# Down and layer 2 on a transposed residual: a four-layer conditioned stack on one NeuronCore

## What is computed

```python
x = x + (einsum('bct,bcd->bdt', x, w0[a]) + bias[a][:, :, None])          # layer 0, 8 tables of 64x64
h = silu(x @ Wg + lora_g(x)) * (x @ Wu + lora_u(x))                       # layer 1, 512 -> 2048, rank 16, adapter a
x = x + (h @ Wd + lora_d(h))                                              #   "down", 2048 -> 512
x = x + (x @ W.T + scal[b] * (x @ A[b].T) @ Bm[b].T)                      # layer 2, 512 -> 512, rank 16, adapter b
x = x + einsum('bct,bcd->bdt', x, w3[c])                                  # layer 3, 200 tables of 64x64
```

## Time and profile before

| | us |
|---|---|
| median of three runs (765.55 to 767.71) | 766.35 |
| the profiled execution, as timed | 767.69 |
| its span, first to last instruction | 765.9 |

### The profile page before, as it was taken

How to read it: one execution, slowest core, us unless ns; L and a number is a source line. 1 busy time by engine, 2 the same in 40 slices (tenths; PEclk the granted TensorE clock), 3 DMA queues, 4 the chain that set the end, 5 groups by cost and what they waited for, 6 DMA issues and landing times.

```text
span 765.9 us, 10652 instructions
## 1 busy us (share of the span) xinstructions
PE 727.8 (95%) x3626; PEld 606.9 (79%) x3626; DVE 601.1 (78%) x1010; ACT 284.8 (37%) x508; POOL 255.3 (33%) x489
## 2 busy tenths in 40 slices
PE   6779889999999999989899999999999999899997
PEld 4547678888888888878778888888888888788886
DVE  7975768797878778799898979787888877766675
ACT  3445523333424333434353334242434333134232
POOL 4724231515223232350327162534425231241100
PEclk9979999999999999999999999999999999999999
DMA  7366520313212121203723232221212061212112
GB/s 209 87 81 194 164 80 29 104 37 108 83 56 83 55 84 56 83 27 111 248 59 109 71 103 73 70 86 58 89 55 85 28 192 32 79 29 70 42 55 83
DMA packets 65941, 66.02 MB, mean 86 GB/s; under 512 B 31712, under 2 KB 48096, under 8 KB 65888
## 3 DMA queue, kind: packets, MB, share of 16 engines
q1 hardware_dynamic: 57248, 45.92, 19.9%
q0 software_dynamic: 7296, 19.41, 8.7%
q10 hardware_dynamic: 1344, 0.02, 0.1%
HBM read 56.94 MB, written 8.39 MB: 85 GB/s over the span
## 4 chain that ended last, share of the span: by engine, by line
PE 84%; DVE 10%; issue 2%; ACT 2%; DMA 1%; POOLq 0%; POOL 0%; ACTq 0%; DVEq 0%
PE bank L1376 36%; PE bank L1474 22%; PE bank L1384 7%; PE bank L1633 6%; PE bank L1483 4%; PE bank L1622 2%; PE bank L1326 1%; PE bank L1599 1%; PE bank L1639 1%; DVE XC L882 1%; PE bank L1650 1%; PE bank L1611 1%; DVE hid L1001 1%; PE bank L1353 1%; DVE hs L1007 1%
## 5 line engine op out<-in xcount | busy, mean ns | idle before, releaser
L1376 PE MATMUL bank<-XC,WC 128*128 128x512 f32 x1344 | 332.9, 394 | 6.7 <-DVE tmp L975 2.2
L1376 PEld LDWEIGHTS bank<-XC,WC 128*128 128x128 f32 x1344 | 245.5, 190 | 54.8 <-issue 4.7
L1474 PE MATMUL bank<-wds,hs 128*128 128x512 f32 x768 | 187.6, 394 | 6.6 <-DVE X L1017 3.3
L1474 PEld LDWEIGHTS bank<-wds,hs 128*128 128x128 f32 x768 | 142.9, 190 | 35.8 <-DVE wds L960 3.8
L398 POOL DMA_INDIRECT BR<-in_L_cond_Bu_dram,boffs x64 | 71.9, 1124 | 265.7 <-DVE BL L954 251.1
L398 POOL DMA_INDIRECT BR<-in_L_cond_Bg_dram,boffs x64 | 76.1, 1189 | 95.2 <-DVE BL L954 80.2
L620 ACT ACTIVATE hs<-hid 128x512 fp32r<-128x512 f32 x64 | 40.3, 630 | 164.4 <-DVE hid L1001 111.4
L1017 DVE TENSOR_TENSOR X<-bank,X 128x512 f32<-128x512 f32 x128 | 86.5, 686 | 17.5 <-PE bank L1474 15.3
L614 ACT ACTIVATE hid<-hid 128x512 f32<-128x512 f32 x48 | 30.4, 633 | 148.4 <-DVE hid L984 75.9
L1384 PEld LDWEIGHTS bank<-UT,BL 128*128 128x128 f32 x512 | 76.4, 190 | 10.0 <-issue 2.1
L1384 PE MATMUL bank<-UT,BL 128*128 128x256 f32 x512 | 81.9, 283 | 1.3 <-ACT hid L611 1.3
(11 more groups left out here) (152 smaller groups left out, 827.9 us busy)
## 6 DMA issues: line engine op xcount, KB each, us to landing
RW<-in_L_cond_Wg_dram SPq DMA_DIRECT2D x16, 512.0 KB, 4.4
RW<-in_L_cond_Wu_dram SPq DMA_DIRECT2D x16, 512.0 KB, 5.1
RD<-in_L_cond_Wd_dram SPq DMA_DIRECT2D x16, 512.0 KB, 3.5
out_dram<-XR SPq DMA_DIRECT2D x16, 256.0 KB, 2.0
X<-in_x_dram SPq DMA_DIRECT2D x8, 256.0 KB, 6.2
udp<-in_x_dram SPq DMA_DIRECT2D x8, 256.0 KB, 4.5
x1park<-RD SPq DMA_DIRECT2D x8, 256.0 KB, 4.2
x2park<-X SPq DMA_DIRECT2D x8, 256.0 KB, 2.5
```

Of the source, the lines that this page charges most:

```text
L1376: last = nc.tensor.matmul(psum[:, :], WC[:, t, left, a, k, :], XC[:, right, b, k, :], start=(first and k == 0 and n == 0), stop=(k == 1 an ...
L1474: last = nc.tensor.matmul(psD[j % 2][:, :], hs[:, f, a, j * P:(j + 1) * P], wds[:, f, b, :], start=(f == 0 and n == 0), stop=(f == 1 and n ...
```

## The change

- The residual lies with features on partitions everywhere behind layer 0. `down` swaps its operands (Wd tile as weights, 512 tokens as moving operand), and `evict` adds into XA, which is the transposed x1 that the block products read anyway. `wd_high`, `wd_low`, the Bd splits and the W2, A2 transposes read their raw tile with a step of four floats (`by_feature`), since feature 4o+k sits in block k.
- Layer 2 takes x2 from there: `transposes2` is gone, `xt_high` and `xt_low` split 128x1024 from SBUF; `lora_down` has 12 matmuls of 256 columns in place of 6 of 512.
- Identity in the weights: `add_identity` now runs before any `place_w0`, so all pairs need only a bias (even pairs on ACT, odd ones on DVE); `w2_identity` (unit 15) and `w3_identity` (unit 14) on DVE. `x3_sum` and `y_sum` are gone; `x3_high` and `x3_low` read PSUM, which stays taken until both have read, and `y_out` on ACT copies layer 3's result out.
- `park_x1` stores the transposed tile in pieces of 512 bytes and waits for `xr_copy(p)` (`s_xr`), where it waited for the bias add. `load_d(0)` no longer waits for these stores. T blocks of the first half get their own place in XB. The warm-up is 12 matmuls of 128 columns, and SBUF names change (XR, X1 to XA, XB).

```diff
                 def park_x1(p):
-                    sp.wait_ge(s_x1b, p - HP + 1)
-                    sp.dma_start(x1park[p - HP, :, :], x1s[p % 2]).then_inc(s_x1st[p % 2], 16)
+                    sp.wait_ge(s_xr, p + 1)
+                    at = slice((p - HP) * P, (p - HP + 1) * P)
+                    sp.dma_start(x1park[:, :, at], XB[:, :, at]).then_inc(s_x1st, 16)
...
                         sp.wait_ge(s_tr, PAIRS)
-                        for s in range(2):
-                            sp.wait_ge(s_x1st[s], 16 * HP // 2)
...
                 def place_w0(p, cols):
                     if p == 0:
-                        pool.wait_ge(s_ident, 1)
-                        pool.wait_ge(s_w0, 32)
+                        pool.wait_ge(s_w0i, 1)
                         pool.wait_ge(s_zero, 1)
...
-                for g in range(2):
-                    cols += adapters(8 * g, 8)
-                    for p in range(4 * g, 4 * g + 4):
+                for n, count in ((0, 4), (4, 4), (8, 8)):
+                    cols += adapters(n, count)
+                    for p in range(n // 2, (n + count) // 2):
...
                 def x1_bias(p):
                     act.wait_ge(s_l0, p + 1)
-                    if p == HP:
-                        act.wait_ge(s_x1, HP)
-                    if p >= HP + 2:
+                    if p == 0:
+                        act.wait_ge(s_bias, 1)
+                    if p >= 2:
                         act.wait_ge(s_tr, p - 1)
-                        act.wait_ge(s_x1st[p % 2], 16 * ((p - HP) // 2))
-                    nc.scalar.activation(x1_of(p), psD[p % 2][:, :], ACT.Identity, bias=bias[:, p:p + 1]).then_inc(s_x1b, 1)
...
-                        nc.scalar.activation(wds[:, f, 0, :], RD[:, f, :], ACT.Copy).then_inc(s_wdh, 1)
+                        nc.scalar.activation(wds[:, f, 0, :].rearrange("p (k o) -> p k o", k=KT), by_feature(RD[:, f, :]),
+                                             ACT.Copy).then_inc(s_wdh, 1)
...
                 def xt_high(d):
-                    for q in range(2):
-                        act.wait_ge(c_tr, 2 * d + q + 1)
-                        if d >= 2 and q == 0:
-                            act.wait_ge(c_l2, 2 * d - 2)
-                        nc.scalar.activation(x2t[d % 2][:, 0, :, q * P:(q + 1) * P],
-                                             bank[q][:, :].rearrange("p (k t) -> p k t", k=KT), ACT.Copy).then_inc(c_xh, 1)
+                    act.wait_ge(s_x2, 2 * d + 2)
+                    if d >= 2:
+                        act.wait_ge(c_l2, 2 * d - 2)
+                    nc.scalar.activation(x2t[d % 2][:, 0, :, :], x2_of(d), ACT.Copy).then_inc(c_xh, 1)
...
+                def x3_high(d, q):
+                    act.wait_ge(c_l2, 2 * d + q + 1)
+                    if d >= 2:
+                        act.wait_ge(c_l3, 2 * (d - 2) + q + 1)
+                    nc.scalar.activation(x3s[d % 2][q][:, 0, :], psD[q][:, :], ACT.Copy).then_inc(c_x3h, 1)
...
+                def w3_high(d, q):
+                    if d == 0 and q == 0:
+                        act.wait_ge(s_w3i, 2)
+                    if d >= 1:
+                        act.wait_ge(c_l3, 2 * (d - 1) + q + 1)
+                    for half in range(2):
+                        rows = slice(half * POS, (half + 1) * POS)
+                        last = nc.scalar.activation(w3bd[q][rows, 0, rows], w3raw[rows, 2 * d + q, :], ACT.Copy)
+                    last.then_inc(c_w3h, 1)
...
+                def y_out(d, q):
+                    act.wait_ge(c_l3, 2 * d + q + 1)
+                    if d >= 2:
+                        act.wait_ge(c_out[d % 2][q], 16 * (d // 2))
+                    nc.scalar.activation(y[d % 2][q], psR[q][:, :], ACT.Copy).then_inc(c_y, 1)
...
+                    dve.wait_ge(s_w0, 32)
+                    tab0 = w0tab.rearrange("p c f -> p (c f)").rearrange("p (n d) -> p n d", d=POS)
+                    nc.vector.tensor_tensor(tab0, tab0, ident2[:, :].unsqueeze(1).to_broadcast([P, ADAPTERS, POS]),
+                                            ALU.add).then_inc(s_w0i, 1)
+                def w2_identity():
+                    dve.wait_ge(s_w2ld, 16)
+                    for k in range(KT):
+                        own_block = w2_raw[:, k, k * P:(k + 1) * P]
+                        last = nc.vector.tensor_tensor(own_block, own_block, ident[:, :], ALU.add)
...
+                    at = slice(half * HP, (half + 1) * HP)
+                    nc.vector.tensor_tensor(w3raw[:, at, :], w3raw[:, at, :],
+                                            ident2[:, :].unsqueeze(1).to_broadcast([P, HP, POS]), ALU.add).then_inc(s_w3i, 1)
...
-                def x1_sum(p):
+                def x1_bias(p):
                     dve.wait_ge(s_l0, p + 1)
-                    nc.vector.scalar_tensor_tensor(out=X1[:, p, :], in0=psD[p % 2][:, :], scalar=bias[:, p:p + 1],
-                                                   in1=X1[:, p, :], op0=ALU.add, op1=ALU.add).then_inc(s_x1, 1)
+                    if p >= 2:
+                        dve.wait_ge(s_tr, p - 1)
+                    nc.vector.tensor_scalar(x1s[p % 2], psD[p % 2][:, :], bias[:, p:p + 1], None, ALU.add).then_inc(s_x1[p % 2], 1)
...
+                    if unit == ALL - 2:
+                        w3_identity(0)
+                        w3_identity(1)
+                    if unit == ALL - 1:
+                        w2_identity()
...
                 for d in range(DUOS):
                     if d + 1 < DUOS:
+                        x2_sum(d + 1, 0)
+                        x2_sum(d + 1, 1)
                         xt_low(d + 1)
-                    x3_sum(d, 0)
-                    if d + 2 < DUOS:
-                        x2_sum(d + 2, 0)
-                        x2_sum(d + 2, 1)
-                    if d + 1 == DUOS:
-                        y_sum(d - 1, 0)
-                        x3_low(d, 0)
-                    x3_sum(d, 1)
+                    x3_low(d, 0)
+                    x3_low(d, 1)
                     if d + 1 < DUOS:
                         u2_mask(d + 1)
-                        if d >= 1:
-                            y_sum(d - 1, 0)
-                        x3_low(d, 0)
-                    if d >= 1:
-                        y_sum(d - 1, 1)
-                    x3_low(d, 1)
-                y_sum(DUOS - 1, 0)
-                y_sum(DUOS - 1, 1)
+                    w3_low(d, 0)
...
-                            last = nc.tensor.matmul(psD[j % 2][:, :], hs[:, f, a, j * P:(j + 1) * P], wds[:, f, b, :],
+                            last = nc.tensor.matmul(psD[j % 2][:, :], wds[:, f, a, j % KT * P:(j % KT + 1) * P],
+                                                    hs[:, f, b, j // KT * 512:(j // KT + 1) * 512],
...
+                    at = d % (DUOS // 2) * QT
+                    for m in range(KT):
+                        q = m // 2
+                        if d and m % 2 == 0:
+                            pe.wait_ge(s_x2, 2 * (d - 1) + q + 1)
+                        for n, (a, b) in enumerate(THREE):
+                            last = nc.tensor.matmul((psE, psC)[q][:, m % 2 * QT:(m % 2 + 1) * QT], BDS[d % 2][:, a, m * P:(m + 1) * P],
+                                                    uds[h][:, b, at:at + QT], start=(n == 0), stop=(n == 2))
+                        if m % 2:
+                            last.then_inc(s_lb, 1)
...
-                def transposes2(d):
-                    for q in range(2):
-                        pe.wait_ge(s_x2, 2 * d + q + 1)
-                        if d >= 1:
-                            pe.wait_ge(c_xl, 2 * d + q - 1)
-                        elif q == 0:
-                            pe.wait_ge(s_tl, TABS)
-                        for k in range(KT):
-                            last = nc.tensor.transpose(bank[q][:, k * P:(k + 1) * P], x2_of(d, q)[:, k * P:(k + 1) * P], ident[:, :])
-                        last.then_inc(c_tr, 1)
...
                 def layer2(d, q):
                     if d >= 1:
-                        pe.wait_ge(c_x3, 2 * d + q - 1)
+                        pe.wait_ge(c_x3l, 2 * (d - 1) + q + 1)
...
                 for d in range(DUOS):
-                    if d + 1 < DUOS:
-                        transposes2(d + 1)
-                    layer2(d, 0)
-                    lora_out(d, 0)
-                    if d + 2 < DUOS:
-                        lora_down(d + 2, 0)
-                        lora_down(d + 2, 1)
-                    if d + 1 == DUOS:
-                        layer3(d - 1, 0)
-                    layer2(d, 1)
-                    lora_out(d, 1)
+                    for q in range(2):
+                        layer2(d, q)
+                        lora_out(d, q)
                     if d + 1 < DUOS:
                         lora_in2(d + 1)
-                        if d >= 1:
-                            layer3(d - 1, 0)
+                    if d + 2 < DUOS:
+                        lora_down(d + 2)
```

(1 more changed line is left out.)

308 lines of the change are left out of this document (146 added, 162 removed).

## The result

The changed kernel takes 773.95 us (median of 4 runs, 772.97 to 774.35); the kernel before took 766.5 beside it (765.55 to 767.71). The ratio is 1.0094, with a 95% interval of 1.0077 to 1.0112: 0.9% slower, where 762.7 us had been forecast. The profiled execution took 774.29 us, its span is 772.4 (765.9 before).

The account below looks back on a forecast made before the run. PE was taken to bound the kernel, apart from waits in unit 0 and the passage to layer 2. Terms 0.2 + 3.7 - 3.8 - 5.7 + 1.3 = -4.3, rounded to -3.7, gave 762.7 us; range 758.8 to 767.8.

Parts of the forecast that it names:

- Start, +0.2: Up to the first gate products: W0 placed later, sums moved to ACT, `t3_sum` 0.2 us later (bounds -1.5 and +1.5).
- Unit 0, +3.7: Loads queued behind `park_x1`, which now waits for the transposed tile's copy, come late: 3.7 us lost, bounds +1.5 and +6.
- x 11, +1.0: Unit 0: x for pair 11, queued behind `park_x1(8)`, is issued at 57.1 and lands 4.8 us later, costing 1.0 us.
- `load_u(1)` and x 14, +1.5: Unit 0: both loads stand behind `park_x1(11)`; PE idles 3.2 us before `layer0(14)`, of which 1.5 us count.
- `load_d(0)`, +1.2: Unit 0: a copy (0.60) and a store's issue (0.56) now precede the first Wd load: 1.2 us.
- Strided reads taken at no cost: Wd splits on ACT and DVE: no extra, 1.57 us per unit free as cover; at 1.5 times, 3.6 us at three waits.
- the slow rival: Half-speed strided reads of Wd exceed the free 1.57 us by 0.85 in each of 13 units: 773.7 us, chance 0.13.
- Identity, +0.95: Before unit 15's down: `w2_identity`'s four DVE additions at 0.24 us each lie on the path; `w3_identity` costs nothing.
- Passage, -3.8: From unit 15 to layer 2: 25.8 us become 22.0, including the identity's 0.95, as waits behind the first `evict` go.
- duos, -5.7: Tail: duos 0 to 5 lose eight transposes each (5.0 us together), the last 0.7; a duo takes 11.07 us, PE bound.
- end, +1.3: After the last `lora_out`: 8.1 us of `layer3`, `y_out`, W3 splitting and store, where 6.8 stood before.
- The clock rival: Unit 0: after the expected 3.2 us idle PE's clock falls, losing 1.9 us: 764.6 us, chance 0.22.

Follow-up runs that it names:

- e12: Changed kernel with the load of the second unit's up weights moved behind x for pair 15; 768.65 us, ratio 1.0037 to the kernel before.
- b1: Kernel before with ACT's and DVE's splits of Wd reading every fourth element, nothing else moved; 773.21 us, ratio 1.0075.
- e6: Changed kernel with late loads ahead of parking stores and x1 of the last four pairs in other buffers, so the first Wd load starts early; 763.55 us, ratio 0.9954.
- e7: e6 with DVE adding the identity to W2 after the last unit's Wd and adapter splits instead of ahead; 762.78 us, ratio 0.9945.
- e4: e5 with Wd split in memory order and PE's weight loads taking every fourth element instead; 769.15 us, ratio 1.0039.
- e5: Changed kernel with loads of up weights, x 14, x 15 and the first Wd block ahead of parking stores; 765.47 us, ratio 0.9984.
- b2: Kernel before with two waits added on SP's queue, delaying `load_u(1)`, x 14 and 15, and `load_d(0)`; 770.34 us, ratio 1.0056.
- b3: Kernel before with both the strided Wd splits of b1 and the late loads of b2; 776.59 us, ratio 1.0137.
- e9: Changed kernel with 28 and 26 needless matmuls of 256 columns on PE in unit 0's two long waits; 769.96 us, ratio 1.0046.
- e13: e7 with every load of x for pairs 10 to 15 ahead of the store it stood behind, no fillers; 762.97 us, ratio 0.9950.
- e11: e13 with needless matmuls on PE in five waits, four at the start and one at the turn; 759.13 us, ratio 0.9901.

## Why the prediction was wrong

**Start, +0.2.** Right as far as it can be told, since the start differs by more than that between executions: first product 0.24 us later (47.03 us, before 46.79), `t3_sum` at 26.92 for 26.70, the first `layer0` at 9.21 for 7.90.

**Unit 0, +3.7.** The mechanism was right, its size was not: +10.0. By its parts:
- x 11, +1.0: nearly nothing (`layer0(11)` starts 0.4 us later, with the start's 0.2 in it). The load was issued at 58.13, later than the 57.1 worked out, but landed in 3.1 us, not 4.8.
- `load_u(1)` and x 14, +1.5: the order and the issue times were met (75.8 worked out, 75.38 measured; idle 3.2, measured 4.22). The wrong term is the landing of 4.8, a median over loads that had neither the 512 KB nor a store in 512 pieces ahead of them; it was 5.8, and 4.0 in e12 with the 512 KB behind. And the clock fell, which stood among the rivals at 1.9 us with a chance of 0.22, though the wait was forecast at 3.2 us beside a wait of 3.00 after which it had fallen. It cost 2.5 us.
- `load_d(0)`, +1.2: right for SP (from `transposes(15)` on PE to the issue 1.87 us, 0.68 before). What failed is that the chain behind it was taken at its old length. The splits in it are 1 us longer on ACT, and the clock falls a second time behind the wait (4.43 us from 102.25 to the down products, 2.45 before: 2.0).

**Strided reads taken at no cost.** This step failed outright, and most clearly: 1.8 times on ACT, 1.57 on DVE, where "I take no extra cost" stood and 1.5 times had been the worst row looked at. b1 prices it at 5.8 us (ratio 1.0075). The cover held in nearly all steady units: the slow rival (every unit 0.85 us late) did not come about. By its own criterion it should have, since the extra is 2 x (0.50 + 0.39) = 1.8 us a unit and 1.57 were free. It took the extras of ACT and DVE as one sum, and they overlap: in unit 14 of the changed kernel ACT's two splits end at 626.7 us, DVE starts its own at 626.86, and only DVE's 0.8 counts. Of the 1.57 us some 0.5 are left (third sum ended at 633.4, product at 633.93). What was missed is where there is no cover. I named three waits and 3.6 us and left them out of the sum; b1 shows five (the three grew by 2.0 us together, the other two by 1.45). The other two are for the adapters' split (`ads`), which stands behind Wd's on DVE, at 174.64 and 409.07 us; at the first the kernel before waits 0.29 us already, a sign of no cover that I passed over, and b1 waits DVE's 0.8 more. The same read was priced on PE by one row of weight loads, 1.5 times at 128 columns of one kind; PE's own strided load of another kind is 1.64 times (311 for 190). "No row shows it" should have meant a middle value in the sum, not zero.

The Trainium skill's sentence on lines of 16 bytes ("Advanced Engine Details and Errata", "Memory Cachelines") pointed the right way; the trace agrees, with 1125 for 622 ns on ACT, 1079 for 689 on DVE and 311 for 190 on PE's weight load.

**Identity, +0.95.** DVE needs 0.80 us (658.49 to 659.29 in its timeline) for W2's four additions; the effect of moving them could not be told from nothing (e6 against e7). PE's wait ahead of unit 15's down grew from 0.26 to 1.45 us. b1, with the step and without the additions, has 1.05 there, so the step is 0.8 of it and the identity an estimated 0.4.

**Passage, -3.8; duos, -5.7; end, +1.3.** Right in the main: -3.9, -5.2 and +1.1, together -8.0 for -8.2. From unit 15's down to layer 2 are 21.90 us (22.0 worked out), before 25.81, but part of this match is luck: the 22.0 holds the identity's 0.95, which lies in the wait ahead of this stretch, and the four groups of down matmuls and ranks took 13.6 us where 12.8 stood. A steady duo takes 11.06 us (11.07 worked out); what is missing of the -5.7 is mostly in the first duo, which takes 10.23 us (10.50 before) with a wait of 0.27 us of its own. From the end of the last `lora_out` to the end are 7.9 us, where 8.1 stood and the terms written out add up to 8.0. Counting matmuls at 0.227 and 0.12 us was enough where PE is the only bound.

**Rivals.** The time came out at 774, which is where the slower rival stood (773.7), but by another way: that rival had every steady unit late, and none was. The clock rival and the 1.5-fold reads at the waits both came true, together and on top of a longer wait; each had been priced alone, 764.6 and 766.3. Their sum with two falls of the clock, 762.7 + 3.6 + 3.8 = 770.1, would have been above the range. (The chance of faster adds up to 0.55 from its cases, not 0.56.)

## What to carry to other kernels

A late load, a slower split behind it and a clock that falls after the wait are one price: rivals that meet in one wait should be added up before the chances are given. A wait put on a shared DMA queue delays every load behind it, and a large transfer issued just ahead of an urgent one delays it again; e12 got 5 us back by moving one load behind two others. And a strided operand is to be priced on every engine that could take it: of the two places tried here, ACT with DVE cost about 6 us (b1, with a fall of the clock in it) and PE more (e4 takes 3.7 us more than e5).

## What the runs showed of the hardware

- A step of four floats costs the same whether it is in the read or, as a step of 128, in the write: 1125 against 1143 ns on ACT, 1079 against 1108 on DVE, packed 622 and 689.
- A weight load with that step takes 311 ns for 190, and PE's 512-column matmuls beside it grow from 394 to 404 ns.
- PE's granted clock is at half for 6.85 us with waits of 4.22 and 4.06 us. It did not fall with 2.48 and 2.60 us (x 14 in b2, b3) and fell with 1.84 and 1.03 us in a row (b2) and 1.52 and 1.03 (e9), and, with the same waits of 0.7 and 1.3 us, the product behind took 1.66 us in e7 and 2.44 in e13. What decides it here is left open, and so a trace of one execution does not tell whether a given wait brings it down.
- Work that nobody needs can pay: 54 matmuls took about 4 us off the changed kernel, and 65 fillers 3.8 off e13 (e11).
